# A recurrent scan with an expert layer on one core: ScalarE's preparation of a later half in four places instead of one

## The reference

```python
dt = soft_clamp(softplus(x @ Wdt.T + bdt), 0.001, 0.1, 0.5)
B_param, C_param = x @ WB.T, x @ WC.T                  # 16 states
A = -exp(soft_clamp(A_log, -5.0, 5.0, 0.5))
dA = exp(soft_clamp(dt[..., None] * A, -8.0, 8.0, 0.5))
def step(h, inp):                                      # 1024 times
    h = dAt * h + dBt * xt[..., None]                  # h: 4 x 256 x 16
    h_norm = sqrt(sum(h * h, axis=(1, 2)))
    h = h * minimum(20.0 / (h_norm + 1e-08), 1.0)
    y = einsum('bdn,bn->bd', h, Ct) + Dp * xt
...
# second branch: 8 experts, top 2, at most 1280 rows each
h = gelu(exp_batches @ c_fc); exp_out = h @ c_proj
...
out = x + s * silu(ffn(xn))
```

## Time and profile before

| | |
|---|---|
| median of three runs | 1704.61 us |
| the profiled execution | 1704.6 us |
| its span, first to last instruction | 1702.6 us |
| busy TensorE / VectorE / ScalarE / POOL | 1291.1 / 1549.6 / 1225.1 / 770.4 us |
| granted TensorE clock, mean | 0.867 |

### The profile page before, as it was taken

How to read it: one execution, slowest core, us unless ns; L and a number is a source line. 1 busy time by engine, 2 the same in 40 slices (tenths; PEclk the granted TensorE clock), 3 DMA queues, 4 the chain that set the end, 5 groups by cost and what they waited for, 6 DMA issues and landing times.

```text
span 1702.6 us, 33871 instructions
## 1 busy us (share of the span) xinstructions
PE 1291.1 (76%) x9356; PEld 1136.9 (67%) x9356; DVE 1549.6 (91%) x9454; ACT 1225.1 (72%) x3152; POOL 770.4 (45%) x1254
## 2 busy tenths in 40 slices
PE   5864435297979797997979798897979798855661
PEld 5753324286868686886868687796878687744551
DVE  6688888899999999998999899999989999987778
ACT  3697548278787887868787887878787777756451
POOL 3156666543434344343444344343434434468842
PEclk8576767698989899998989999898989899877785
DMA  9931111210111021021002002011101110012245
GB/s 332 340 127 47 44 41 44 95 36 17 51 49 46 17 77 31 18 62 50 28 24 86 24 26 75 25 39 37 63 18 34 66 32 20 20 44 71 75 127 202
DMA packets 95533, 113.29 MB, mean 67 GB/s; under 512 B 8432, under 2 KB 85360, under 8 KB 95344
## 3 DMA queue, kind: packets, MB, share of 16 engines
q1 hardware_dynamic: 87696, 94.13, 17.0%
q0 software_dynamic: 6144, 16.79, 3.1%
q10 hardware_dynamic: 1504, 0.22, 0.1%
HBM read 60.91 MB, written 50.20 MB: 65 GB/s over the span
## 4 chain that ended last, share of the span: by engine, by line
PE 54%; DVE 14%; ACT 12%; issue 7%; POOL 7%; DMA 4%; SPq 1%; POOLq 0%; ACTq 0%; DVEq 0%
PE ps L1210 15%; PE ps L1194 13%; PE ps L1182 10%; PE ps L1176 6%; ACT arena L870 4%; POOL arena L531 4%; DVE arena L751 3%; POOL xg L511 3%; PE ps L1141 3%; PE ps L1157 3%; DVE arena L722 2%; DVE arena L728 2%; DVE arena L740 2%; DVE arena L736 2%; ACT arena L858 2%
## 5 line engine op out<-in xcount | busy, mean ns | idle before, releaser
L531 POOL TENSOR_TENSOR arena<-arena,neghalf 128x1 f32<-128x1 f32 x1025 | 591.8, 577 | 851.2 <-DVE arena L725 780.3
L751 DVE SCALAR_TENSOR_TENSOR arena<-arena 128x128 f32<-128x128 f32 x1024 | 361.6, 353 | 54.0 <-POOL arena L531 53.6
L1182 PE MATMUL ps<-arena,pick 128*128 128x128 f32 x2048 | 301.9, 294 | 38.8 <-ACT arena L966 19.8
L736 DVE CUSTOM_DVE_ANT_0 arena<-arena 128x128 f32<-128x128 f32 x1024 | 294.0, 287 | 30.3 <-ACT arena L966 25.4
L1176 PE MATMUL ps<-ident,arena 128*128 128x128 f32 x1024 | 210.7, 333 | 137.6 <-ACT arena L870 132.0
L966 ACT ACTIVATE arena<-ps,arena 128x128 f32<-128x128 f32 x1024 | 291.4, 376 | 32.8 <-PE ps L1182 32.8
L1182 PEld LDWEIGHTS ps<-arena,pick 128*128 128x128 f32 x2048 | 280.2, 211 | 50.9 <-ACT arena L966 38.0
L1194 PE MATMUL ps<-arena,wf 128*128 128x256 f32 x1280 | 302.0, 386 | 8.1 <-issue 8.1
L728 DVE CUSTOM_DVE_ANT_0 arena<-arena 128x128 f32<-128x128 f32 x1024 | 299.0, 292 | 0.0
L1210 PE MATMUL ps<-wp,arena 128*128 128x256 f32 x1280 | 295.8, 385 | 2.6 <-ACT arena L974 2.3
L1176 PEld LDWEIGHTS ps<-ident,arena 128*128 128x128 f32 x1024 | 179.9, 244 | 167.4 <-ACT arena L870 137.2
(11 more groups left out here) (146 smaller groups left out, 1379.7 us busy)
## 6 DMA issues: line engine op xcount, KB each, us to landing
xg<-zeros SPq DMA_DIRECT2D x10, 1024.0 KB, 9.6
xrow<-xg SPq DMA_DIRECT2D x40, 256.0 KB, 2.7
yg<-arena SPq DMA_DIRECT2D x40, 256.0 KB, 2.2
arena<-in_x SPq DMA_DIRECT2D x16, 512.0 KB, 9.3
wf<-in_c_fc SPq DMA_DIRECT2D x8, 1024.0 KB, 5.0
wp<-in_c_proj SPq DMA_DIRECT2D x8, 1024.0 KB, 6.0
arena<-dx SPq DMA_DIRECT2D x66, 64.0 KB, 2.4
ys<-arena SPq DMA_DIRECT2D x66, 64.0 KB
```

Source lines behind the costliest of these rows:

```text
L531: g.tensor_tensor(sv[:, slot, 1:2], mx, neghalf[:, 0:1], ALU.pow).then_inc(s_ready, 1)
L736: v.tensor_tensor_reduce(out=junk[:, 1, :], in0=vv, in1=vv, scale=1.0 / CLAMP ** 2, scalar=0.0, op0=ALU.mult, op1=ALU.add, accum_out=ac[:, ...
L751: v.scalar_tensor_tensor(hr[:, slot, :], vv, sv[:, before, 1:2], ur[:, slot, :], ALU.mult, ALU.add)\
L1182: last = t.matmul(ps[2][:, j * P:(j + 1) * P], pick[:, q * QUAD + j, :], xin, start=True, stop=True)
```

## The change

A half h is prepared while an earlier group of four blocks is being fed. Before, TensorE's time_rates and ScalarE's logs_of stood at the end of the group three halves ahead (the last quad of its last block), logs_of right behind the exponentials of decay_ops; b_and_c and b_and_c_out came in quad (0,1) of the next group, that is quad 1 of its block 0; squares_of at the end of the block 0 after that, its sums in quad (1,0). Now time_rates and logs_of stand in quad (0,1), b_and_c and b_and_c_out in (1,1), squares_of at the end of block 1 and its sums in quad (2,0). VectorE's addition of the logs moves one block later.

```diff
-            for table, pieces, lo_, hi_ in ((sum_at, 1, 4 * h - 8, 4 * h - 6), (input_at, 2, 4 * h - 5, 4 * h - 3), (norm_at, 1, 4 * h - 2, 4 * h)):
+            for table, pieces, lo_, hi_ in ((sum_at, 1, 4 * h - 7, 4 * h - 5), (input_at, 2, 4 * h - 5, 4 * h - 3), (norm_at, 1, 4 * h - 2, 4 * h)):
...
-                    if blk % 4 == 0 and blk > 0 and q == 1 and blk // 4 + 2 < HALVES:
+                    if blk % 4 == 1 and q == 1 and blk // 4 + 2 < HALVES:
                         b_and_c_out(blk // 4 + 2, 6)
-                    if blk % 4 == 1 and q == 0 and 2 <= blk // 4 + 1 < HALVES:
+                    if blk % 4 == 2 and q == 0 and 2 <= blk // 4 + 1 < HALVES:
                         sums_out(blk // 4 + 1, 6)
...
-                    if blk == 0 and q == 1:
-                        logs_of(2, 6)
-                    if blk == 0 and q == 2:
-                        b_and_c_out(2, 6)
-                if blk % 4 == 3 and blk + 4 < NBLK:
-                    if (blk + 9) // 4 < HALVES:
-                        logs_of((blk + 9) // 4, 6)
+                    if blk % 4 == 0 and q == 1 and blk // 4 + 2 < HALVES:
+                        logs_of(blk // 4 + 2, 6)
                 if blk % 4 == 2 and blk // 4 + 2 < HALVES:
                     soft_clamp(blk // 4 + 2)
-                if blk % 4 == 0 and 2 <= blk // 4 + 1 < HALVES:
+                if blk % 4 == 1 and 2 <= blk // 4 + 1 < HALVES:
                     squares_of(blk // 4 + 1)
...
-                    h = {(3, 3): blk // 4 + 3, (0, 1): blk // 4 + 2, (1, 0): blk // 4 + 1}.get((blk % 4, q), 0)
-                    if blk == 0:
-                        h = {1: 2, 2: 2}.get(q, 0)
+                    h = {(0, 1): blk // 4 + 2, (1, 1): blk // 4 + 2, (2, 0): blk // 4 + 1}.get((blk % 4, q), 0)
```

More of the change, by code:

```diff
@@ L1221, in _ @@
                         after_evictions()
-                        if blk % 4 == 3 or (blk == 0 and q == 1):
+                        if blk % 4 == 0:
                             pe.wait_ge(xch_in[h // 2 % 2], 16 * ((h // 2 + 1) // 2))
@@ L1225, in _ @@
                             waiting = [z_used, h + 1]
-                        elif blk % 4 == 0:
+                        elif blk % 4 == 1:
                             b_and_c(h, 6)
```

## The result

The changed kernel takes 1751.43 us, the median of four runs (1746.48 to 1755.02), against 1704.8 for the kernel before on the same chips: a ratio of 1.027, 95% interval 1.0243 to 1.0297. It is slower by 46.6 us, as forecast in sign; the forecast of 31.1 us was a third too small. The profiled execution took 1746.48 us, the fastest of the four, span 1744.5.

The account below looks back on a forecast made before the run. TensorE, waiting for ScalarE, was taken to pace groups 3 to 13. Terms -4.5 + 5.2 + 14.3 + 5.0 + 5.2 + 3.6 + 2.3 = 31.1 us on 1704.6 gave 1735.7 us; range 1710 to 1756, forecast case 1712 to 1748.

Parts of the forecast that it names:

- already covered: At a group's start, TensorE is busy with quad (0,0) while ScalarE does the logarithms, so they take nothing from TensorE.
- the rival "heavier": Each of ten new waits drops the clock, 1748 us; further waits in (0,3) and (1,0), up to 1770; chance 0.17.
- (a): Logarithms off the lump: TensorE's short waits for the windows at a group's first quads shrink, -4.5 us.
- (b): Time-rate products leave quad (3,3) for (0,1): exponentials start 1.25 us earlier, TensorE pays 1.91 us; +5.2 us.
- (c): Behind quad (0,1), ScalarE's 6.9 us block outlasts TensorE's work, so (0,3)'s input products wait: +14.3 us (0 to 30).
- (d): Quad (0,3), five groups: expert products wait for quad (0,2)'s gelu, now behind a table load; +5.0 us (0 to 9).
- (e): Quads (1,1) and (2,0): moved products behind a turn wait for ScalarE's turned rows, four times; +5.2 us (0 to 7).
- (f): Waits in groups 6, 9 and 11 drop TensorE's clock, one old drop goes; two more drops, +3.6 us (0 to 18).
- Step (g): VectorE meets the chain's late quad at (0,2) instead of (0,0): +2.3 us, once.
- The rival "faster": The lump itself paces; moving its logarithms removes all 21.7 us of VectorE's waits, about 1683 us; chance 0.08.

Follow-up runs that it names:

- the last run: Kernel before with time rates behind the next block's inputs, one table set at the lump, quad (0,0)'s expert products ahead of the exponentials' wait: 1679.92 us, ratio 0.9853.
- The fill that failed: Kernel before with only quad (0,0)'s expert products moved ahead of TensorE's wait for the exponentials, in groups without a turn there: 1713.63 us, ratio 1.0048.

## Why the prediction was right, and where its sum fell short

The sign and the mechanism hold. TensorE waits for ScalarE and not for VectorE, before and after; ScalarE's block behind quad (0,1) is 6.97 us long and TensorE waits behind it in (0,3), in all of groups 3 to 13. One argument for it was worth less than it seemed: that TensorE's busy time and waits fill the stretch speaks against no rival, since they do so in the last run as well. What shows the pace before is that VectorE waits for ScalarE, and that the time rates moved on TensorE alone gave 14.6 us. That the logarithms in the lump were "already covered" holds less well: eleven of their loads taken out there gave 8.6 us between the traces and 12.9 between the medians, where the prediction had seen 4.5 us of waits for the windows. The time itself, 1751, lies past the 1748 us up to which the forecast reached, in what the rival "heavier" named: part of it happened, the further waits in (1,0) and more time at a low clock. By its own steps, from the two lists of waits, for groups 3 to 13:

| step | predicted | measured | from |
|---|---|---|---|
| (a) windows | -4.5 | -4.0 | L920: 5.7 to 1.7 |
| (b) time rates | +5.2 | +2.7 | L870 +4.1; on L978 2.1 to 0.7 |
| (c) wait in (0,3) | +14.3 | +19.3 | L966: 1.6 to 20.9 |
| (d) gelu | +5.0 | +3.1 | L974: 2.3 to 3.9 + 1.5 |
| (e) turned rows | +5.2 | +5.8 | 1.7 to 5.3 + 2.2 |
| (f) clock | +3.6 | +9.8 | busy 926.98 to 936.79 |
| (none) wait in (1,0) | 0 | +9.6 | L912: 9.3 to 18.9 |
| other | 0 | -0.7 | |

The measured column adds up to 45.6 of the 45.8 us. That (e) came out so near is in part luck: four waits of 1.3 us were forecast, and the new ones are three of 0.74, one of 2.02 and one of 3.27. The steps that failed in size:

- **The missing row.** The prediction's sum ended with the gelu of quad (0,3); waits in (1,0) stood only in a rival, without a cause. It had counted the table loads, but not where the third and fourth stand: where quad (0,2) ends in a down, Tanh comes first, loads its own set, and Gelu's load follows, so that ScalarE stays late for another quad (groups 4, 7, 10, 12 and 13; the wait grew in the last four). The order of the program showed it. Gelu's set loaded once took 9.1 us off, 4.3 of it in these waits; the run without tables took them back to 10.1, near the 9.3 of before.
- **(c)** was low because what was taken for covered was not: groups 3, 4, 7 and 10 had 1.3 for the wait and got about 1.6, and group 11 4.4 where 3.0 stood. Group 13 has the block as well and was left out of the sum; it waits 1.62.
- **(f)** The prediction let three waits drop the clock and one drop go. TensorE's busy time grew by 9.8 us with the same instructions, and seven stretches at half clock stand where two did: 26.3 us of work at half clock lose 13.2, 6.8 lost 3.4, and the difference is the 9.8. The work at half clock around the group starts is nearly as before (47.7 us and 48.1).
- **(b)** was high: the wait at L870 was to grow by 1.91 - 1.25 = 0.66 at each start, and grew by 0.38 at seven, 0.72 at two and not at two. At group 6 the time rates took 1.75 us of TensorE's row, from 671.18 to the next start at 672.93, and without them ScalarE's load ahead of the exponentials came 1.37 earlier: 2.35 us behind the start of the time rates before, 0.98 behind that of the transpose that follows now.

Step (g), where VectorE meets the chain, shows in its waits: of the 50.5 us on L966, 37.8 stand ahead of quad (0,2), as forecast, and 10.5 still at a group's last step; 12 more waits end with TensorE's L1136, at block starts. No run separates it from the rest.

The rival "faster" put its chance on the lump as such. Moving nothing on ScalarE, but the time rates on TensorE, took 14.6 us off; the lump can stay where it is.

## What to carry to other kernels

Before breaking up a lump on one engine, look at what another engine does meanwhile: work that is covered where it stands can be uncovered by moving it, and its price there is the part by which it, with every table switch that the new neighbours bring, outlasts the work beside it. Here that was the table loads: without tables TensorE hardly waited for the block. Where two engines hand work to and fro, list the waits of each over a stretch and what ended them; the chain that never waits for the third engine, while that one waits for it, is the one to shorten, and work of its own can be put into its longest wait. That busy time and waits add up to the stretch is no sign by itself. The fill that failed shows the limit: taking work out of a cover exposes what it covered.

## What was not expected of the hardware

A switch of table sets cost between about 0.2 us and nearly its full 1.28 by its place alone: 3.4 us for 20 of them ahead of a wait, 17.5 us for 14 in the path. A wait of TensorE of 2.87 us was followed by a stretch at a granted 0.50, in which eight products took 1.82 us and 16 took 4.60, where 1.06 and 3.62 stand in the kernel before at the same place, so the short wait cost 1.7 us on top of itself. It is not so each time. The wait of 2.31 us behind which the earlier trace rows show a down at half clock stands in the changed kernel too, and there the 16 products behind it take 3.72 us, at a granted 1.00; behind a wait of 2.80 in group 12 no drop shows either:

```profile
758.34 3.72 PE L1205 MATMUL ps<-wp,arena 128*128 128x256 f32 x16 [2.31 <-ACT arena L974]
```

Behind a wait of 1.75 us in group 13 the clock fell, though the prediction saw no drop behind waits of up to 1.8. What decides it stays open.
